# Gather-bound message passing on one core: SP's row fetches handed to POOL, and features loaded for four pairs at once

## What is computed

```
h    = relu(layernorm(x))                          # 6250 x 128
W    = silu(edge_attr @ fw1 + fb1) @ fw2 + fb2     # 206250 x 50 -> 206250 x 128
t    = silu(h @ aw1 + ab1) @ aw2 + ab2             # the node table, 6250 x 128
msg  = W * t[src]                                  # one 512-byte row of the table per edge
agg  = segment_sum(msg, dst)                       # 6250 x 128
out  = x + h + silu(agg @ ow1 + ob1) @ ow2 + ob2
```

## Time and profile before

| what | value |
|---|---|
| median of the runs | 1909.62 us |
| the profiled execution's own time | 1909.67 us |
| its span, first to last instruction | 1907.9 us |
| PE busy | 1694.2 us (89%) |
| DVE busy | 1497.8 us (79%) |
| POOL busy | 1429.2 us (75%) |
| ACT busy | 357.4 us (19%) |
| granted TensorE clock, mean | 0.955 of full speed |

### The profile page before, as it was taken

One profiled execution on the slowest core, in us unless ns is written; L12 is line 12 of the kernel. 1 busy time (PEld: TensorE's weight loads), 2 busy tenths in 40 slices (PEclk: granted clock), 3 DMA queues, 4 the chain that ended last, 5 costly groups with the idle time before them and its releaser, 6 DMA issues.

```text
span 1907.9 us, 30563 instructions
## 1 busy us (share of the span) xinstructions
PE 1694.2 (89%) x9385; PEld 1035.1 (54%) x9385; DVE 1497.8 (79%) x2779; ACT 357.4 (19%) x442; POOL 1429.2 (75%) x1499
## 2 busy tenths in 40 slices
PE   4456898999999999999999899899898898998855
PEld 3344555555565655556555565565554555555544
DVE  7598667869878788888887799787777776787755
ACT  4332121222222221111111111111111111111110
POOL 7677777777777777777777777777777777777775
PEclk9787999999999999999999999999999999999976
DMA  5643332332333333333333233333233233233321
GB/s 193 203 119 92 93 89 75 93 97 77 93 99 93 86 94 92 97 93 99 98 87 93 77 99 92 96 103 83 86 95 91 74 96 95 70 97 90 90 80 52
DMA packets 84582, 182.24 MB, mean 96 GB/s; under 512 B 29824, under 2 KB 43264, under 8 KB 84416
## 3 DMA queue, kind: packets, MB, share of 16 engines
q0 software_dynamic: 47744, 97.88, 19.3%
q10 hardware_dynamic: 24096, 69.22, 11.0%
q1 hardware_dynamic: 12576, 13.17, 2.1%
HBM read 170.51 MB, written 9.63 MB: 94 GB/s over the span
## 4 chain that ended last, share of the span: by engine, by line
POOL 57%; PE 19%; issue 19%; DVE 2%; DMA 2%; ACT 1%; POOLq 0%; SPq 0%; ACTq 0%; DVEq 0%
POOL xg L485 57%; PE banks L1188 9%; PE banks L1145 4%; PE banks L1132 2%; PE banks L1077 1%; DMA node_table<-res 1%; PE banks L1197 1%; PE banks L1073 1%; DMA xg<-node_table,src 0%; DVE sums L877 0%; PE banks L1068 0%; PE banks L1062 0%; PE banks L1084 0%; ACT hs L624 0%; PE banks L1157 0%
## 5 line engine op out<-in xcount | busy, mean ns | idle before, releaser
L485 POOL DMA_INDIRECT xg<-node_table,src x1444 | 1382.1, 957 | 447.2 <-issue 438.8
L1188 PE MATMUL banks<-spare,parts 128*128 128x512 bf16 x3528 | 795.7, 381 | 3.6 <-DVE spare L909 3.6
L1188 PEld LDWEIGHTS banks<-spare,parts 128*128 128x128 bf16 x3528 | 348.6, 100 | 383.6 <-issue 12.2
L877 DVE TENSOR_REDUCE sums<-banks 128x128 f32<-128x1024 f32 (+1 forms) x408 | 494.0, 1211 | 13.6
L550 ACT ACTIVATE hid<-banks,cols 128x1024 f32<-128x1024 f32 x202 | 224.5, 1111 | 1299.1 <-PE banks L1132 1266.1
L1145 PEld LDWEIGHTS banks<-wts,hid 128*128 128x128 f32 x3224 | 454.2, 204 | 15.5
L1145 PE MATMUL banks<-wts,hid 128*128 128x128 f32 x3224 | 452.1, 286 | 0.0
L874 DVE TENSOR_TENSOR banks<-banks,xg 128x1024 f32<-128x1024 f32 (+1 forms) x183 | 221.7, 1212 | 278.0 <-DMA xg<-node_table,src 269.8
L909 DVE TENSOR_SCALAR spare<-sel_marks 128x512 bf16<-128x512 bf16 x1176 | 277.8, 304 | 55.3 <-PE banks L1145 54.5
L1077 PE MATMUL banks<-bias_rows,ones_b 128*128 128x512 bf16 (+1 forms) x429 | 172.1, 401 | 107.5 <-DVE sums L877 107.3
L881 DVE TENSOR_TENSOR banks<-banks,other 128x1024 f32<-128x1024 f32 (+1 forms) x204 | 248.7, 1219 | 7.0
(11 more groups left out here) (111 smaller groups left out, 465.9 us busy)
## 6 DMA issues: line engine op xcount, KB each, us to landing
attr<-in_attr ACTq DMA_DIRECT2D x67, 768.0 KB
e_x<-node_table SPq DMA_DIRECT2D x2048, 0.5 KB
xg<-node_table,src POOLq DMA_INDIRECT x1444, 2.5
row_first<-node_table SPq DMA_DIRECT2D x1024, 0.5 KB
sel_src<-in_sel_src ACTq DMA_DIRECT2D x24, 256.0 KB
hs<-node_table ACTq DMA_DIRECT2D x6, 512.0 KB, 4.1
resid_s<-residual ACTq DMA_DIRECT2D x8, 256.0 KB, 2.7
out<-res ACTq DMA_DIRECT2D x8, 256.0 KB
```

Source lines behind the costliest of these rows:

```text
L485: pool.indirect_dma_start(xg[:, i % XG, j, :], None, table[:, :], bass.IndirectOffsetOnAxis(ap=src[:, s * L + j:s * L + j + 1], axis=0))\
L877: return dve.reduce_sum(sums[:, at, m, :], of.rearrange("p j f -> p f j"), AX.X)
L1188: step = pe.matmul(sel_ps, parts[:, m, k, :], sel_hot[:, s % 2, i, :], start=k == 0 and m == 0, stop=last)
```

## The change

The three row pairs become main pairs: turns 64, 118 and 184 are now in `MAIN_TURNS`, which has 184 entries, and POOL gathers them like all the others, through `xg`. SP's fetches, the buffer `row_first`, the list `row_src`, its load (L413) and its scaling on DVE (L855) are gone. `PART` is 4 and no longer 3: `attr` has two halves of four pairs each, every load brings four pairs (1024 KB and no longer 768 KB), and `features` is called at every fourth pair. The selected pairs and the early pairs stay as they are.

```diff
 XG = 3
 SETS = 4
-PART = 3
+PART = 4
...
-ROW_TURNS = (64, 118, 184)
-ROW_TILES = (L, L, L)
-ROW_SLOTS = (None, 0, 1)
...
-MAIN_TURNS = [s for s in range(PAIRS) if s not in EARLY_TURNS + SEL_TURNS + ROW_TURNS]
+MAIN_TURNS = [s for s in range(PAIRS) if s not in EARLY_TURNS + SEL_TURNS]
...
-        row_first = sb("row_first", [P, L, F])
...
-            sp.dma_start(row_src, row_src_t).then_inc(row_src_in, 16)
...
-            sp.wait_ge(row_scaled, 1)
-            for m in range(ROW_PAIRS):
-                if ROW_SLOTS[m] is not None:
-                    sp.wait_ge(msg_done, run(EARLY_TURNS[ROW_SLOTS[m]]))
-                for q in range(ROW_TILES[m] * P // ROWS_AT_ONCE):
-                    begins = begins_of(sp, m, q)
-                    for i, begin in enumerate(begins):
-                        row_transfer(sp, m, q, i, begin)
...
-            dve.wait_ge(row_src_in, 16)
-            dve.tensor_scalar(row_src, row_src, float(ROW_BYTES), None, ALU.mult).then_inc(row_scaled, 1)
...
-                elif s in ROW_OF:
-                    m = ROW_OF[s]
-                    rows_of = row_x(m)
-                    for landed in row_in[m]:
-                        dve.wait_ge(landed, 16 * ROW_TILES[m] * P // ROW_SIGNALS)
```

More of the change, by code:

```diff
@@ L87 @@
 EARLY_TURNS = tuple(SEL_TURNS[r] + SEL_STEP // 2 + 3 for r in range(EARLY_PAIRS))
-MAIN_TURNS = [s for s in range(PAIRS) if s not in EARLY_TURNS + SEL_TURNS + ROW_TURNS]
-assert len(MAIN_TURNS) == PAIRS - len(EARLY_TURNS + SEL_TURNS + ROW_TURNS)
+MAIN_TURNS = [s for s in range(PAIRS) if s not in EARLY_TURNS + SEL_TURNS]
+assert len(MAIN_TURNS) == PAIRS - len(EARLY_TURNS + SEL_TURNS)
 MAIN_OF = {s: i for i, s in enumerate(MAIN_TURNS)}
@@ L219, in after, with gnn_layer @@
     return run(s + FILL)
-def gnn_layer(nc, x, e_src_t, src_t, sel_src_t, row_src_t, dst_t, attr_t, node_wts_t, wts_t, cols_t, rows_t, out):
+def gnn_layer(nc, x, e_src_t, src_t, sel_src_t, dst_t, attr_t, node_wts_t, wts_t, cols_t, rows_t, out):
     f32, i32, bf16, u8 = mybir.dt.float32, mybir.dt.int32, mybir.dt.bfloat16, mybir.dt.uint8
@@ L226, in gnn_layer @@
     table = nc.dram_tensor("node_table", [NODE_TILES * P, F], f32).ap()
-    table_bytes = table.bitcast(u8).rearrange("(o n) b -> o (n b)", o=1)
     resid = nc.dram_tensor("residual", [NODE_TILES * P, F], f32).ap()
@@ L284, in gnn_layer @@
         onehot = sb("onehot", [P, OH_SETS, 2, WIN])
-        row_src = moments.rearrange("p m t -> p (m t)")[0:L * P // ROWS_AT_ONCE, 0:ROW_PAIRS * ROWS_AT_ONCE].bitcast(i32)
-        row_first = sb("row_first", [P, L, F])
         e_x = sb("e_x", [P, EARLY_PAIRS * L, F])
@@ L299, in gnn_layer @@
         sel_T = hT[:, GC:2 * GC]
-        def row_x(m):
-            return row_first[:, :, :] if ROW_SLOTS[m] is None else e_x[:, ROW_SLOTS[m] * L:(ROW_SLOTS[m] + 1) * L, :]
         spare = sb("spare", [P, max(3 * EDGE_TILES // 2 + 4 * PAIRS, SEL_MOST * GC)])
@@ L354, in gnn_layer @@
         half_gathered = [sem(f"half_gathered{i}") for i in range(2 * len(HALVED))]
-        row_rest = sem("row_rest")
-        row_src_in, row_scaled = sem("row_src_in"), sem("row_scaled")
-        row_in = [[sem(f"row_in{m}_{i}") for i in range(ROW_SIGNALS)] for m in range(ROW_PAIRS)]
         e_gathered = [sem(f"e_gathered{r}") for r in range(EARLY_PAIRS)]
@@ L374, in gnn_layer @@
         a_l1, a_mid, a_l2, a_res, a_out = (sem(n) for n in ("a_l1", "a_mid", "a_l2", "a_res", "a_out"))
[L376 to L384, removed]
         def edges_left(eng):
@@ L468, in _ @@
             pool.wait_ge(s_tab, 16 * (AHEAD + table_writes(N_CHUNKS - 1)))
[L470 to L475, removed]
             for i, s in enumerate(MAIN_TURNS):
-                for m, r in enumerate(ROW_TURNS):
-                    if ROW_TILES[m] < L and MAIN_TURNS[i - 1] < r < s:
-                        rest_of_rows(m)
                 if i >= XG:
@@ L960, in pair @@
                     dve.wait_ge(job_taken, job_done(("second", 2 * r + 1)))
-                elif s in ROW_OF:
-                    m = ROW_OF[s]
-                    rows_of = row_x(m)
-                    for landed in row_in[m]:
-                        dve.wait_ge(landed, 16 * ROW_TILES[m] * P // ROW_SIGNALS)
-                    if ROW_TILES[m] < L:
-                        dve.wait_ge(row_rest, 16 * sum(L - n for n in ROW_TILES[:m + 1]))
                 elif s in SEL_OF:
@@ L1288 @@
     attr[:, :NG] = features.reshape(PAIRS, P, 2, TPG, NG).transpose(2, 4, 0, 3, 1).reshape(2, NG, PAIRS * GC)
-    row_src = np.zeros((L * P // ROWS_AT_ONCE, ROW_PAIRS, ROWS_AT_ONCE), src_p.dtype)
-    for m, s in enumerate(ROW_TURNS):
-        nodes = src_p[s, :, :ROW_TILES[m]].reshape(-1, ROWS_AT_ONCE)
-        row_src[:len(nodes), m] = nodes
-    row_src = row_src.reshape(-1, ROW_PAIRS * ROWS_AT_ONCE)
     arrays = {
@@ L1298 @@
         "sel_src": np.ascontiguousarray(src_p[list(SEL_TURNS)].reshape(SEL_PAIRS, P, 2, TPG).transpose(0, 2, 3, 1).reshape(SEL_HALVES, GC)),
-        "row_src": row_src,
         "dst": np.ascontiguousarray(dst_p.transpose(1, 0, 2).reshape(P, EDGE_TILES)),
```

## The result

The changed kernel took 1939.01 us (median of 5 runs) where the kernel before, run beside it, took 1909.37: ratio 1.0156, interval [1.0144, 1.0168], so +29.8 us [27.5, 32.1]. The forecast was 1939.0.

A forecast was written before the change was run, and what follows sets the result against it. The prediction took POOL's unbroken gathers, each followed by a fixed pause, as the bound: +30.0 us for 24 gathers, -2.0 for a wait gone, +1.3 at the start, +29.3 in all, giving 1939.0 us, range 1935 to 1943.

The forecast's parts named there:

- The bound: Main gathers: POOL works without a break, its idle time being a fixed 305 ns pause after each gather; pitch 1.262 us.
- The price of a gather: POOL's 24 added gathers each cost the median plus the pause, 0.944 + 0.305 = 1.249 us, together +30.0 us.
- The wait at pair 75: POOL's one real wait for DVE, at 750.67 us, goes once pair 64's gathers make POOL later: -2.0 us.
- The start: Larger first feature loads delay the sixth chunk's table write and POOL's first gather, to 72.2 us: +1.3 us.
- SP, DVE's scaling, the features in the edge stage: Removing SP's fetches and DVE's scaling, and shrinking PE's 9.6 us wait for features, gains 0; SP at most 1.4 us.
- The sum: Whole kernel: +30.0 - 2.0 + 1.3 = +29.3 us, giving 1939.0 us.
- What I said the trace would show: 1468 gathers, mean 956 to 957 ns; POOL's wait about 1 us; DVE's wait +25 us; chain through POOL in one piece.
- Pair 64 is hidden: From 440 to 786 us PE hides pair 64's eight gathers, so only +21.3 us, 1931 us; chance 0.04.
- slow gathers are SP's: SP's issues or traffic lengthen gathers; without them all fall to 938 ns, 1909 to 1910 us; chance 0.02.
- PE's clock: PE at its lower clock level becomes the bound for stretches, two of 5 us loss: 1949 us; chance 0.05.
- Lock-out: DVE instructions block POOL's added gathers, each at the longest duration: 42.9 us, 1952 us; chance 0.03.

The follow-up runs named there:

- after_defer: The changed kernel with ACT's first two feature loads issued only after the last table write has landed; 1932.55 us, ratio to the kernel before 1.0131.
- after_again: The changed kernel unaltered, submitted a second time for a trace at the usual clock; 1937.39 us, ratio to the kernel before 1.0154.
- part3: The changed kernel with features loaded for three pairs at once, as before, so only the gathers are changed; 1937.24 us, ratio to the kernel before 1.0148.
- pair64: The kernel before with pair 64 alone gathered by POOL, SP still fetching pairs 118 and 184; 1915.47 us, ratio 1.0038.
- late_pairs: The kernel before with pairs 118 and 184 gathered by POOL, SP still fetching pair 64; 1928.58 us, ratio 1.0109.
- no_fetch: The kernel before without SP's 3072 row fetches and without gathers in their place, so those rows are left out; 1908.46 us, ratio 0.9998.
- before_defer: The kernel before with ACT's first two feature loads issued only after the last table write has landed; 1906.02 us, ratio 0.9985.
- few_selectors2: The changed kernel with one selector made in each turn, selected rows wrong, second try, on a slower chip; ratio 0.9644 to the kernel before there.
- four_rows_defer2: The kernel before with a fourth pair, 150, fetched by SP and the first two feature loads deferred, second try, slower chip; 2889.53 us, ratio 1.0839.

## Why the prediction was right, point by point

**The bound.** Right. In the eight traces with a time of 1908 to 1942 us POOL issues without a break, but for at most one real wait, at pair 75, and each pair handed to it is paid: +7.3 us for pair 64 (10.0 less the wait of 2.0), +20.8 for two, +28.2 for all three without the feature change.

**The price of a gather.** Right in size. With gathers at a median of 944 ns, as before, `after_defer` has 1916.03 - 65.17 = 1850.86 us from first to last start, 27.7 more than before; the forecast for this distance was 30.0 - 2.0 = 28.0. `after_again` and `part3`, with a median of 947, have 1854.48 and 1854.75; less 1467 x 3 ns = 4.4 us they are at 1850.1 and 1850.4, +26.9 and +27.2. Also right is that the added gathers cost the median and not the mean: the gathers over 970 ns number 196 in the trace of before, 197 in `after_again`, 193 in `pair64` and 202 in `after_defer`, with 18 to 20 us of excess in each (the 191 of the expectations is the count from 975 ns on). Their number did not grow with the gathers.

**The wait at pair 75.** Right: it goes as soon as pair 64 is POOL's (0.3 us at most in `pair64` and in the changed kernel) and stays without it (1.00 in `late_pairs` and `no_fetch`). Its size is less steady than I took it: over the pause it is 2.0 us in `before`, 0.7 in `late_pairs` and `no_fetch`, and 3.2 in `before_defer`, where POOL starts sooner. The way there was milder than I had it: I put DVE 3 to 5 us behind at pairs 64 and 65, and against before it was 1.4 us late at pair 65 and 2.1 us early at pair 72.

**The start.** The mis-sized term. I had +1.3 us, first gather at 72.2 us; it was at 69.47. Most of that is upstream of the change: the sixth chunk's write was issued at 56.53 us, before at 58.46, and this moment lies between 56.5 and 58.5 in the six traces that have the write on their chain. From that write to the first gather it took 12.94 us; in the five traces with the small loads 12.38, 12.58, 12.40, 11.69 and 12.34, mean 12.28. That puts the larger loads at +0.7 us, half the forecast, by one trace against five that differ by 0.9 among themselves; that they cost anything is not shown. I had let the write end with the loads' last byte in both cases at 386 GB/s; in `after_again` the six us from 58 to 64 moved 409 GB/s, and the small-load landings alone differ by 0.9 us (7.46 to 8.35). The fit that the prediction quotes from the Trainium skill ("DMA: Bandwidth & Descriptors", Anatomy of one DMA) is given there for DMAs that GpSimd issues. These loads are ACT's, and nothing in the sum hangs on it.

**SP, DVE's scaling, the features in the edge stage.** Right at 0 within 1 to 2 us: `no_fetch` is 0.9998 [0.9989, 1.0007] of before, and the features' 9.6 us of PE's waiting went without a gain that shows (`part3` has them back). The feature loads fall from 68 to 51, not from 67.

**The sum.** At gathers of 944 ns it is some +27.5 for the distance and perhaps +0.7 for the start, 28.2 us, where I had 29.3 and the two submissions gave 29.8 and 29.4, with intervals of 2.4 us to either side. So the agreement to 0.01 us is luck; right to 2 us is what is shown.

**What I said the trace would show.** The wait on DVE, the pause and the distance over 1845 us came. DVE's wait for gathers grew by 57.3 us and not 25: I had kept DVE's other waits as they were, but its wait for PE's filters at the selectors fell from 54.5 to 32.9 us, and it waits for rows in its place: 21.6 of the 32 us that I missed. And the chain is not in one piece on POOL: it still takes 11% over PE, up to a gather at 615.62 us that DVE's message released 0.30 us before it, no later than the pause would have let it go. A chain follows the last releaser even when it came in time to the hundredth. So it was before the change, where I read the chain's way over PE as passing through the wait at 750.67 us. It doesn't: the chain leaves POOL at the tie at 801.23 us and is on PE when POOL waits at 750.67. The chain of the kernel before:

```profile
799.99 1.15 DVE banks L874
801.14 0.09 issue
801.23 0.94 POOL xg L485
```

The 2.0 us were read from the wait itself and not from the chain, and `pair64` bears them out (+7.3 us where 10.0 - 2.0 was expected).

**The rivals.** "Pair 64 is hidden" fell with `pair64`, "slow gathers are SP's" with `no_fetch`. "PE's clock" fell in `after_again` (0.3 us of waiting, mean granted clock 0.951, before 0.955). "Lock-out" at its full price, 1952 us, fell with the time and with the slow gathers' constant number. That DVE's selectors lengthen the gathers that they meet is supported by the count above, at 16.5 / 380, or 43 ns for each such gather.

## What to carry to other kernels

An engine that is 75% busy can be the bound: look for a pause after each of its instructions that waits for nothing, and for how little it waits for others. Then an added instruction costs its pitch, busy and pause, and what shortens another engine's work brings nothing by itself. Before that loop starts, look at which loads were put beside its last input: moving two of them back was worth 2.9 us on the kernel before and 4 to 5 us on the changed one.

## What the runs showed of the hardware that I had not expected

- POOL's gathers have one of two median lengths in an execution. The medians are 944 ns in `before`, `pair64`, `late_pairs`, `after_defer` and `no_fetch`, and 947 in `after_again`, `part3` and `before_defer`. The kernel doesn't decide it: the changed kernel has 947 in `after_again` and 944 in the trace of the first submission. Over 1444 gathers 3 ns are 4.3 us, about the spread between runs of one kernel (1906.32 to 1911.49 for before). ACT's large activation goes from 1113 to 1114 ns with it on the first chip (elsewhere `few_selectors2` and `four_rows_defer2` have 944 with 1114), and DVE's reduction is 1224 ns in both. The cause stays open.
- The same kernel took 1909 us on one chip and 2664 and 2668 on two others. There the mean granted clock is lower (0.82 to 0.83 for before, where the first chip has 0.95), and PE issues single matmuls with gaps that nothing in the profile ends. PE in order of time in `few_selectors2`:

```profile
992.88 0.36 PE L1090 MATMUL banks<-wts,hid 128*128 128x128 f32 x1 [0.58 <-issue]
994.29 0.27 PE L1090 MATMUL banks<-wts,hid 128*128 128x128 f32 x1 [1.05 <-issue]
995.69 0.38 PE L1090 MATMUL banks<-wts,hid 128*128 128x128 f32 x2 [1.13 <-issue]
```

  SP's issues slow down alike (710 us for 1024 rows), while POOL's gathers keep their 944 ns. What holds PE's and SP's instructions back stays open.
